# Linear attention with a routed expert layer on one core: a quad's state steps and both inter-chunk sets as one group ahead of its first scores

## What is computed

```python
xn = layernorm(x)
q, k, v = split(xn @ W_qkv)                 # 16 heads of 8
k = layernorm over each head (no affine)
for each chunk of 64 tokens of a sequence:  # S starts at 0, one 8x8 state per head
    inter  = S applied to q_c
    scores = where(causal, q_c k_c^T, 0)
    out_c  = inter + scores v_c
    S      = S + v_c k_c^T
attn = out @ W_o
# feed-forward: each token goes to the one of 8 experts whose centroid fits best
e = argmax(xn @ centroids^T); a = sigmoid(of that product)
y = a * (xn + W2[e] relu(W1[e] (ln(xn) * g[e] + b[e]) + b1[e]) + b2[e]) + (1 - a) * xn
out = x + attn + y
```

## Time and profile before

| | us |
|---|---|
| median of 3 runs | 363.37 |
| lowest and highest run | 362.53, 364.1 |
| span of the profiled execution, from first to last instruction | 362.3 |
| span to first `scores` | 12.95 |
| the 15 quads from first `scores` of quad 0 to that of quad 15 | 193.09 |
| PE, DVE, ACT, POOL busy in the span | 341.5, 283.4, 242.3, 250.6 |

### The profile page before, as it was taken

How to read it: one execution, slowest core, us unless ns; L and a number is a source line. 1 busy time by engine, 2 the same in 40 slices (tenths; PEclk the granted TensorE clock), 3 DMA queues, 4 the chain that set the end, 5 groups by cost and what they waited for, 6 DMA issues and landing times.

```text
span 362.3 us, 17501 instructions
## 1 busy us (share of the span) xinstructions
PE 341.5 (94%) x6868; PEld 293.6 (81%) x6868; DVE 283.4 (78%) x799; ACT 242.3 (67%) x657; POOL 250.6 (69%) x245
## 2 busy tenths in 40 slices
PE   7798999989999999999999989999999999999991
PEld 6466787767687687778868878999999999999990
DVE  8887898897785887977878786788877778777760
ACT  4787687777577667666665735766777767766660
POOL 3488477898797865455555503888888888888884
PEclk9999999999999999999999999999999999999997
DMA  7220333536314031445453435555555555555420
GB/s 196 70 62 19 105 91 112 178 104 187 105 48 120 26 99 52 149 131 159 132 158 94 133 86 144 67 74 71 69 69 71 72 73 69 71 76 60 36 24 0
DMA packets 55153, 33.18 MB, mean 92 GB/s; under 512 B 5352, under 2 KB 52768, under 8 KB 55072
## 3 DMA queue, kind: packets, MB, share of 16 engines
q1 hardware_dynamic: 42800, 23.53, 23.5%
q0 software_dynamic: 12272, 8.54, 17.1%
HBM read 18.72 MB, written 13.78 MB: 90 GB/s over the span
## 4 chain that ended last, share of the span: by engine, by line
issue 26%; PE 18%; POOL 12%; DVE 1%; ACT 1%; POOLq 1%; DVEq 0%; ACTq 0%
POOL out_dram L494 12%; PE sc L1274 4%; PE bank L1328 3%; PE bank L1337 2%; PE bank L1222 2%; PE bank L1200 1%; PE bank L1306 1%; PE bank L1295 1%; PE bank L1209 1%; PE bank L1215 1%; POOLq L71 1%; PE bank L1255 1%; DVE pr L856 1%; PE bank L1228 1%; PE bank L1233 1%
## 5 line engine op out<-in xcount | busy, mean ns | idle before, releaser
L494 POOL DMA_INDIRECT out_dram<-qx,rows x71 | 112.7, 1588 | 36.2 <-issue 21.9
L694 ACT ACTIVATE qx<-sc,b1T 128x128 f32<-128x128 f32 x280 | 80.0, 368 | 39.6 <-PE sc L1421 39.4
L420 POOL DMA_INDIRECT slots_d<-rows,pos_i x64 | 63.1, 986 | 40.6 <-PE bank L1328 10.3
L856 DVE TENSOR_TENSOR pr<-sc,causal 128x1536 f32<-128x1536 f32 (+2 forms) x33 | 63.5, 1926 | 16.1 <-PE sc L1274 16.0
L1429 PE MATMUL bank<-tokens,qx 128*128 128x128 f32 x568 | 75.2, 275 | 0.7 <-ACT qx L694 0.7
L1421 PE MATMUL sc<-wide,tokens 128*128 128x128 f32 x560 | 74.0, 275 | 0.5 <-issue 0.5
L1429 PEld LDWEIGHTS bank<-tokens,qx 128*128 128x128 f32 x568 | 69.0, 192 | 1.1 <-ACT qx L694 1.1
L1421 PEld LDWEIGHTS sc<-wide,tokens 128*128 128x128 f32 x560 | 68.2, 192 | 0.6 <-issue 0.6
L1015 DVE COPY tokens<-xT 128x1024 f32 x71 | 52.8, 745 | 0.0
L1030 DVE SCALAR_TENSOR_TENSOR qx<-bank,rows,qx 128x128 f32<-128x128 f32 x71 | 24.8, 349 | 27.2 <-PE bank L1429 26.2
L1274 PEld LDWEIGHTS sc<-qx,kT 32*64 32x64 f32 x2048 | 32.9, 130 | 15.5 <-issue 15.0
(11 more groups left out here) (167 smaller groups left out, 530.7 us busy)
## 6 DMA issues: line engine op xcount, KB each, us to landing
rows<-slots_d SPq DMA_DIRECT2D x71, 66.0 KB, 2.1
res<-in_L_attn_x_dram SPq DMA_DIRECT2D x16, 256.0 KB
out_dram<-res SPq DMA_DIRECT2D x16, 256.0 KB, 3.6
tokens<-in_L_attn_x_dram SPq DMA_DIRECT2D x7, 512.0 KB, 4.2
w1raw<-in_L_ffn_w_dram SPq DMA_DIRECT2D x8, 256.0 KB
w2raw<-in_L_ffn_w_dram SPq DMA_DIRECT2D x8, 256.0 KB
out_dram<-qx,rows POOLq DMA_INDIRECT x71, 3.4
slots_d<-rows,pos_i POOLq DMA_INDIRECT x64
```

What stands on the lines that cost most here:

```text
L420: pool.indirect_dma_start(slots_d, bass.IndirectOffsetOnAxis(ap=pos_i[:, t:t + 1], axis=0), rows[:, t, :], None)\
L494: pool.indirect_dma_start(out_rows, bass.IndirectOffsetOnAxis(ap=xs[:, a, D + 2:D + 3].bitcast(U32), axis=0), ye[:, a, :], None, bounds_ch ...
L694: last = nc.scalar.activation(ht[:, k % 2, c * P:(c + 1) * P], inner(k)[:, c * P:(c + 1) * P], ACT.Relu, bias=b1T[:, bass.ds(e * FC + c, 1)])
L856: nc.vector.tensor_tensor(pr[:, h % 2, a:G, w].rearrange("p g (j t) -> p g j t", t=CH), sc[:, a * BANK:G * BANK].rearrange("p (g w) -> p g ...
```

## The change

Each quad's loop on TensorE is written in another order. `state_step(n + 1)`, `inter_second(n)` and `inter_first(n + 1)`, all on 64x64 tiles, now stand next to each other just ahead of `scores(2n + 2)`; `kT_project(n + 2)` is done a quad earlier, behind `v_project` and `output`; `k_transpose` and `q_project` follow `products(2n - 1)`. So the full-width products of a quad stand in two groups. The state steps of both chunks go into `FA` and `FB`, now one tensor `fab`, and one DVE instruction (`dstate_copy`, 128x512) masks both, ahead of `score_mask(2n)` instead of behind it. Tokens and weights are turned in the score banks `XA` = `SC[2]` and `XB` = `SC[3]`, which have to be read out first. ACT copies q once and expands it from SBUF, and its loop is reordered; POOL's state work stands ahead of `mask_scores`, and its late `send_rows` come in bursts of two and five. The diff, cut to its core:

```diff
-        banks = [ctx.enter_context(nc.psum_tensor(f"bank{i}", [P, BANK], F32)) for i in range(4)]
-        FA, FB, Y = banks[0], banks[1], banks[2:4]
+        fab = ctx.enter_context(nc.psum_tensor("fab", [P, 2 * BANK], F32))
+        FA, FB = fab[:, 0:BANK], fab[:, BANK:2 * BANK]
+        banks = [FA, FB]
+        Y = [ctx.enter_context(nc.psum_tensor(f"y_bank{i}", [P, BANK], F32)) for i in range(2)]
+        XA, XB = SC[2], SC[3]
...
+                if h % 2 == 0 and h:
                     state_middle(n)
                     state_end(n)
+                mask_scores(h)
+                if h == 0:
+                    state_middle(0)
+                    state_end(0)
+                if h % 2 == 0:
...
-            for h in range(ROUTED, NH):
-                n = h // 2
-                pool.wait_ge(s("sc_ps"), h + 1)
-                send_rows(1)
-                if h % 2 == 0:
-                    pool.wait_ge(s("av_ps"), h)
-                    send_rows(1)
-                    if n + 1 < NQ:
-                        pool.wait_ge(s("q_ps"), n + 2)
-                        send_rows(1)
-                elif n + 1 < NQ:
-                    pool.wait_ge(s("v_ps"), n + 2)
-                    send_rows(1)
-                    pool.wait_ge(s("out_ps"), n)
-                    send_rows(1)
-                    pool.wait_ge(s("w2_ps"), n - 6)
-                    send_rows(1)
+            for n in range(LATE, NQ):
+                pool.wait_ge(s("av_ps"), 2 * n)
+                send_rows(2)
+                pool.wait_ge(s("av_ps"), 2 * n + 1)
+                send_rows(5)
...
-                    act.wait_ge(s("q_ps"), n + 1)
+                    act.wait_ge(s("qT_sb") if n else s("q_ps"), n + 1)
                     reach(act, s("sc_ps"), 2 * (n - 1))
-                ins = nc.scalar.activation(qx[:, n % 2, :, j, :], FA[:, :].rearrange("p (i t) -> p i t", t=P), ACT.Copy,
+                q = qT[:, n % 2, :] if n else FA
+                ins = nc.scalar.activation(qx[:, n % 2, :, j, :], q.rearrange("p (i t) -> p i t", t=P), ACT.Copy,
                                            scale=gmask[:, j * DK:j * DK + 1])
                 if j == J - 1:
                     ins.then_inc(s("qx_sb"), 1)
             def q_copy(n):
+                act.wait_ge(s("q_ps"), n + 1)
                 reach(act, s("inter_ps"), n - 1)
-                nc.scalar.activation(qT[:, n % 2, :], FA[:, :], ACT.Copy).then_inc(s("qT_sb"), 1)
+                nc.scalar.activation(qT[:, n % 2, :], FA, ACT.Copy).then_inc(s("qT_sb"), 1)
...
+            kT_copy(1)
             for h in range(NH):
                 n = h // 2
                 more = n + 1 < NQ
                 norm = n + 1 < NCH
-                if h % 2 and more:
-                    q_expand(n + 1, 0)
-                    q_expand(n + 1, 1)
-                if h and by_act(h):
-                    score_copy(h)
                 if h % 2 == 0:
-                    if more:
-                        kT_copy(n + 1)
+                    if h and by_act(h):
+                        score_copy(h)
                     if norm:
                         ln_root(n + 2)
                     if n:
...
                     if more:
                         kn_copy(n + 1)
                         k_square(n + 1)
-                    if norm:
-                        ln_norm(n + 2, (5, 6))
+                        q_copy(n + 1)
+                        q_expand(n + 1, 0)
                     if n in (2, 4, 6, 8):
                         second_root(n // 2 - 1)
                 else:
                     if more:
                         k_root(n + 1)
-                        for j in range(2, J):
-                            q_expand(n + 1, j)
+                        q_expand(n + 1, 1)
+                    if by_act(h):
+                        score_copy(h)
+                    if norm:
+                        ln_norm(n + 2, (5, 6))
+                    if more:
+                        q_expand(n + 1, 2)
+                        q_expand(n + 1, 3)
                     if n < 8 and n % 2 == 1:
                         affT_copy(n // 2)
-                    if more:
-                        q_copy(n + 1)
-                    if more:
-                        values_across(n + 1)
+                    if n and n + 2 < NQ:
+                        kT_copy(n + 2)
                     if norm:
-                        xT_copy(2 * n + 2, FA)
-                        xT_copy(2 * n + 3, FB)
+                        xT_copy(2 * n + 2, XA)
+                        xT_copy(2 * n + 3, XB)
                     elif n - 7 < E:
                         w1_copy(n - 7)
                         w2_copy(n - 7)
+                    if n == 0:
+                        kT_copy(2)
+                    if more:
+                        values_across(n + 1)
...
-            def dstate_first(n):
+            def dstate_copy(n):
                 dve.wait_ge(s("ds_ps"), n + 1)
                 reach(dve, s("smid_ready"), n)
-                nc.vector.tensor_tensor(dstate[:, 0, :, :], Y[n % 2][:, 0:HALF * GW].rearrange("p (i k) -> p i k", k=GW),
-                                        bcast(smask[:, :], 1, HALF), ALU.mult).then_inc(s("dsta_sb"), 1)
-            def dstate_second(n):
-                reach(dve, s("state_ready"), n)
-                nc.vector.tensor_tensor(dstate[:, 1, :, :], FA[:, 0:HALF * GW].rearrange("p (i k) -> p i k", k=GW),
-                                        bcast(smask[:, :], 1, HALF), ALU.mult).then_inc(s("dstb_sb"), 1)
+                reach(dve, s("state_ready"), min(n, NQ - 2))
+                chunks = NC if n < NQ - 2 else 1
+                nc.vector.tensor_tensor(dstate[:, 0:chunks, :, :],
+                                        fab[:, :].rearrange("p (c w) -> p c w", w=BANK)[:, 0:chunks, 0:HALF * GW]
+                                        .rearrange("p c (i k) -> p c i k", k=GW),
+                                        bcast(bcast(smask[:, :], 1, HALF), 1, chunks), ALU.mult).then_inc(s("dst_sb"), 1)
...
+                    if n:
+                        dstate_copy(n)
+                    score_mask(h)
+                    if n == 0:
+                        dstate_copy(n)
                     if n == NQ - 1:
                         b1_fold(E - 1)
-                        dstate_first(n)
-                        score_mask(h)
-                    else:
-                        score_mask(h)
-                        dstate_first(n)
-                    if n < NQ - 2:
-                        dstate_second(n)
...
+            def turned(n):
+                if n + 1 < NCH:
+                    pe.wait_ge(s("xT_sb"), 2 * n + 4)
+                elif n - 7 < E:
+                    pe.wait_ge(s("w1_sb"), n - 6)
+                    pe.wait_ge(s("w2_sb"), n - 6)
...
-                    second_left(n - 2)
+                    pe.wait_ge(s("qT_sb"), n)
                 pe.wait_ge(s("xT_sb"), n + 1)
-                mm(FB[:, :], wqkv[:, D:2 * D], xT[:, HALF * n:HALF * (n + 1), :].rearrange("p i t -> p (i t)"), start=True,
+                mm(FB if n < 2 else FA, wqkv[:, D:2 * D], xT[:, HALF * n:HALF * (n + 1), :].rearrange("p i t -> p (i t)"), start=True,
                    stop=True).then_inc(s("kT_ps"), 1)
             def k_transpose(n):
                 pe.wait_ge(s("kT_sb"), n + 1)
+                if n:
+                    pe.wait_ge(s("dst_sb"), n)
...
-                bank_y_free(n)
-                if n == 0:
-                    pe.wait_ge(s("qT_sb"), 1)
-                    pe.wait_ge(s("xT_sb"), 2)
-                else:
-                    first_left(n - 1)
-                if n == 1:
-                    pe.wait_ge(s("small_sb"), 2)
-                if n in (3, 5, 7, 9):
-                    rank_tokens(n // 2 - 1)
+                pe.wait_ge(s("qT_sb"), n + 1)
+                pe.wait_ge(s("kT_sb"), min(n + 2, NQ))
                 for i in range(HALF):
                     for a in range(P // GW):
-                        for c, bank in ((0, Y[n % 2]), (1, FA))[:2 if n < NQ - 2 else 1]:
+                        for c, bank in ((0, FA), (1, FB))[:2 if n < NQ - 2 else 1]:
...
+                    if n:
+                        turned(n - 1)
...
-                    pe.wait_ge(s("dsta_sb"), n + 1)
+                    bank_y_free(n)
...
+                pe.wait_ge(s("dst_sb"), 2 * b + 4)
...
-            for h in range(NH):
-                n = h // 2
+            for n in range(NQ):
                 more = n + 1 < NQ
                 norm = n + 1 < NCH
-                scores(h)
-                if h % 2 == 0:
-                    if more:
-                        kT_project(n + 1)
-                    state_step(n)
-                    if h:
-                        products(h - 1)
-                    inter_first(n)
-                    if more:
-                        k_transpose(n + 1)
-                    if n and out_early(n):
-                        output(n - 1)
```

(60 more changed lines are left out.)

34 lines of the change are left out of this document (13 added, 21 removed).

## The result

| | before | after |
|---|---|---|
| median, us | 363.63 (4 runs) | 384.06 (381.29 to 385.89, 4 runs) |
| ratio | | 1.0565, interval 1.0524 to 1.0605 |
| span of the profiled execution | 362.3 | 379.6 |
| first `scores` to first `scores` of quad 15 | 193.09 | 209.02 |
| from there to the first expert product | 11.68 | 13.33 |

The account below looks back on a forecast made before the run. TensorE's own order was taken as the bound; +4.1, +3.4, -0.1, -1.4 and -0.3 gave +5.7, less 1.9 for interruptions: +3.8, span 366.1, median 367.2 us (1.1% slower). Range 360.5 to 373, the forecast's own 364.5 to 370.5.

Parts of the forecast that it names:

- The reading of the bound: From quad 2 on TensorE's own order of groups sets the time; TensorE is busy for 94% of the span.
- the first quad: Quad 0: `state_step(0)` waits for `kT_copy(1)`, the later chain follows; an inter set ends at 29.0 instead of 25.1, +3.9 us.
- the price of one shape change: On TensorE, a change of tile shape between groups costs 0.10 us; a quad has seven instead of eleven.
- the list of what would show it: Five signs for the profile after, among them first scores of quad 2 near 29, not 25.
- The interruptions: Five halts of TensorE inside product groups, about 5.0 us before; half of the three early ones (3.8) taken off: -1.9.
- the saving of 6.0: Fewer shape changes on TensorE save 0.4 us a quad, 6.0 for 15 quads, if PE stays the bound.
- the term of +3.4: Quads 2 to 5: PE waits for ACT's key copy ahead of the state step; 50.8 us becomes 54.2.
- that term's mechanism: Quads 10 to 13: PE's state step waits for DVE's `v_scale`, starting at 10.8; the quad ends at 12.4 us.
- The mask between a quad's scores: First to second scores: PE has 3.7 us, before 6.0; the late mask needs 3.8, costing 0.1 within the 12.4.
- PE stays the bound: Rival: 0.4 us a quad comes through, waits on ACT do not bind; 357.4, or 359.6 with first-quad loss; chance 0.15.
- The waits chain: Rival: late `kT_copy` delays ACT further in each of quads 1 to 7, or POOL is late; 373 to 375; chance 0.13.
- None of the four: PE stays the bound (0.15), no change at 362 to 365 (0.20), the waits chain (0.13), the forecast at 364.5 to 370.5 (0.52).

Follow-up runs that it names:

- the light kernel: The changed kernel with half of the scores' and values' short products left out (scores from the second quad on): 364.18 us, ratio 1.0003 to before.

## Why the prediction was wrong

**What held.** The reading of the bound (PE's own order), the first quad and the price of one shape change. TensorE's timeline in the first quad:

```profile
17.67 0.69 PE L1245 MATMUL fab<-vp,kn 64*64 64x64 f32 x32 [2.42 <-ACT kT L589]
19.26 0.63 PE L1213 MATMUL fab<-ident,kT 128*128 128x128 f32 x4 [0.90 <-DVE dstate L867]
...
26.37 1.10 PE L1205 MATMUL fab<-xT,wqkv 128*128 128x512 f32 x2 [0.93 <-ACT xT L519]
28.25 0.69 PE L1245 MATMUL fab<-vp,kn 64*64 64x64 f32 x32 [0.78 <-ACT kT L589]
...
29.34 1.21 PE L1266 MATMUL sc<-qx,kT 32*64 32x128 f32 x64
```

The second quad's first scores stand at 29.34, forecast 29.0 (the list of what would show it calls this quad 2; by its own working it is quad 1). The term of +3.9 is right by 0.3. `v_project`, now ahead of a full-width group:

```profile
51.12 1.16 PE L1220 MATMUL fab<-wqkv,xT 128*128 128x128 f32 x8
52.11 1.06 PE L1330 MATMUL y_bank<-wo,y 128*128 128x128 f32 x8
53.01 1.02 PE L1205 MATMUL fab<-xT,wqkv 128*128 128x512 f32 x2
```

It takes 0.99, and `output` 0.90, 0.10 and 0.09 less than before.

**The step that failed** is the last of the sum: "The interruptions were 5.0 and may be anything from 0 to 5 now ... I take off half of the three early ones (3.8): -1.9". They went to 27.0 in the fifteen quads. I had taken five halts that wait for nothing shown as a given amount of noise that waits could hide, and gave their growth no number. It stood in the last sentence as a thing that would make me wrong, with the right reason, but with no chance and no price. Both could have been had from before: all seven halts stood at multiples of 256 records from each other, and within a group of short products (six in `products`, one in `inter_first`). A counted distance would have led to the density.

**Taking the quads apart.** With the halts taken out of either kernel:

| | before | forecast | after |
|---|---|---|---|
| quads 0 and 1 | 25.0 | 29.1 | 29.7 |
| quads 2 to 5 | 50.8 | 54.2 | 49.3 |
| quads 6 to 9 | 50.3 | 50.4 | 47.4 |
| quads 10 to 14 | 61.6 | 60.4 | 55.6 |
| sum | 187.7 | 194.1 | 182.0 |

The span's growth is then -5.7 + 21.6 (halts) + 1.65 (quad 15) - 0.3 (experts) = 17.3. The last column does not mean that PE would take 182.0 without halts: what it shows is that quads with halts hardly wait for anything else. Nor is -5.7 the saving of 6.0 come true: it is +4.7 in quads 0 and 1 and -10.4 in the others, and that the two nearly give the forecast's number is luck. ScalarE in quad 4, and DVE's `k_var` in quads 4 and 10 (their timelines):

```profile
81.28 0.35 ACT L552 ACTIVATE kstd<-kvar,eps 128x64 f32<-128x64 f32 x1 [2.08 <-DVE kvar L828]
...
84.62 0.57 ACT L589 ACTIVATE kT<-fab 128x512 f32<-128x512 f32 x1
```

```profile
80.56 0.69 DVE L828 TENSOR_REDUCE kvar<-sq 128x64 f32<-128x512 f32 x1
...
161.44 0.68 DVE L828 TENSOR_REDUCE kvar<-sq 128x64 f32<-128x512 f32 x1
162.03 2.28 DVE L856 TENSOR_TENSOR pr<-sc,causal 128x2048 f32<-128x2048 f32 x1
164.87 0.69 DVE L843 TENSOR_TENSOR vp<-fab,krs 128x512 f32<-128x512 f32 x1
```

and TensorE's answer in quad 4:

```profile
73.01 0.69 PE L1266 MATMUL sc<-qx,kT 32*64 32x128 f32 x32
...
85.34 0.69 PE L1245 MATMUL fab<-vp,kn 64*64 64x64 f32 x32 [0.63 <-ACT kT L589]
```

The chain is the one forecast: `k_var` 7.55 after the first scores (forecast 6.9), the key copy starts at 11.6 (forecast 10.9), the state step at 12.3 (forecast 11.6). But PE had lost 2.1 us to halts in that quad by then, so the wait left over is 0.63, and in quads 2, 3 and 5 there is none. For the term of +3.4 the place was right and the size was taken by the halts; in the light kernel it comes back in the even quads (1.12 us each in quads 2, 4 and 6, where the forecast had 1.7, 1.7 and 0.9). In the late quads, `v_scale` of quad 10 is done at 165.6, while PE reaches the state step only at 167.06, having halted 1.92 us in `v_project`. No wait for it shows in any late quad, so that term's mechanism was not seen, and 12.4 us for such a quad came to 13.4 to 14.1 by halts.

**The mask between a quad's scores** was right: 3.7 us (158.84 - 155.10) for 3.7 to 3.8.

**Quad 15 and the median.** In the 1.65 us there stand two more halts of 1.3 us together (28.3 - 27.0; before has none there) and a low clock, whose shares were not told apart: the last window above has 0.87 granted, and a group of products takes 1.79 us from start to start instead of 1.03:

```profile
227.66 0.65 PE L1266 MATMUL sc<-qx,kT 32*64 32x128 f32 x18 [0.66 <-issue]
228.24 1.86 PE L1321 MATMUL y_bank<-pr,vz 128*32 128x64 f32 x64
230.03 1.12 PE L1298 MATMUL y_bank<-qT,smid 64*64 64x64 f32 x16
```

Between the profiled execution (381.29) and the median lie 2.8 us, and a difference of the clock beside them: the profiled run had a mean clock of 0.990, the other three 0.973, 0.979 and 0.976 with 385.89, 384.98 and 383.13 us; before, the profiled execution has 0.994. Those runs have no trace of their own, so where their clock was low, and whether it is all of the 2.8, is not shown.

**The rivals.** "PE stays the bound" had its price of a shape change borne out, but no gain came of it. "The waits chain" would have given 373 to 375 by waits on ACT; the view of waits has 3.8 us of them. None of the four was what happened.

## What to carry to other kernels

Idle time that the profile gives to no releaser can have one cause, and needs its rival with a price: count TensorE's records between such halts (products, weight loads and semaphore waits), and where the distance is constant, work out for old and new order how many microseconds of work each block of that size holds. Here that asks for 3.7 us or more of work in 256 records, and for more where a packet starts late; grouping short products to save 0.1 us a shape change took the densest part to 2.5 us and cost some 20 us. Wide groups between short ones are not only work: they are the time in which the next instructions arrive.
